# A state-space block and a mixture of experts on one core: the state's input product made in the router's pass and kept in DRAM

## The reference

```python
u = _rmsnorm(x, ssm_norm_w)
lam = jax.nn.sigmoid(log_lambda)
Bu = jnp.einsum('btd,nd->btn', u, B_w)
def step(h, bu_t):
    h = lam * h + bu_t
    return (h, h)
_, hs = jax.lax.scan(step, h0, jnp.swapaxes(Bu, 0, 1))
hs = jnp.swapaxes(hs, 0, 1)
y = jnp.einsum('btn,dn->btd', hs, C_w) + D_skip * u
x = x + y
z = _rmsnorm(x, ffn_norm_w)
gate = jax.nn.silu(jnp.einsum('btd,fd->btf', z, w1))
val = jnp.einsum('btd,fd->btf', z, w3)
```

## Time and profile before

| | us |
|---|---|
| median of 3 runs (1972.17 to 1979.03) | 1974.25 |
| the profiled execution | 1973.12 |
| its span, first to last instruction | 1971.2 |
| TensorE busy | 1804.0 |
| VectorE busy | 1038.4 |
| ScalarE busy | 652.8 |
| GpSimd busy | 1050.9 |

### The profile page before, as it was taken

One profiled execution on the slowest core, in us unless ns is written; L12 is line 12 of the kernel. 1 busy time (PEld: TensorE's weight loads), 2 busy tenths in 40 slices (PEclk: granted clock), 3 DMA queues, 4 the chain that ended last, 5 costly groups with the idle time before them and its releaser, 6 DMA issues.

```text
span 1971.2 us, 31040 instructions
## 1 busy us (share of the span) xinstructions
PE 1804.0 (92%) x9958; PEld 1346.9 (68%) x9960; DVE 1038.4 (53%) x2462; ACT 652.8 (33%) x1349; POOL 1050.9 (53%) x1057
## 2 busy tenths in 40 slices
PE   6798998999989999999999898888898869999995
PEld 3455555655568888889888787777787845555553
DVE  6587456333234555445455565566565635555554
ACT  5620222222224444444444343334343322222220
POOL 0003777777777777720004644445444157777666
PEclk9898999999989999999999999999999979999998
DMA  6804334563668889875557877777777653333333
GB/s 207 257 10 144 136 127 167 186 231 140 241 219 282 280 282 283 276 215 174 170 176 221 262 237 227 235 233 233 221 233 223 187 156 113 107 109 100 101 96 104
DMA packets 261671, 374.55 MB, mean 190 GB/s; under 512 B 30357, under 2 KB 227081, under 8 KB 260617
## 3 DMA queue, kind: packets, MB, share of 16 engines
q1 hardware_dynamic: 211448, 227.51, 37.5%
q0 software_dynamic: 49920, 145.03, 22.3%
q10 hardware_dynamic: 144, 0.03, 0.0%
HBM read 189.47 MB, written 182.98 MB: 189 GB/s over the span
## 4 chain that ended last, share of the span: by engine, by line
PE 66%; DMA 15%; DVE 12%; issue 3%; SPq 2%; ACT 1%; DVEq 1%; POOL 1%; POOLq 0%; ACTq 0%
PE ps L1155 21%; DMA arena<-sorted_rows 14%; PE ps L1239 14%; PE ps L1172 11%; PE ps L1253 9%; PE ps L1228 5%; DVE arena L1026 2%; DVE xe L940 2%; PE ps L1141 1%; PE ps L1112 1%; PE ps L1079 1%; PE ps L1128 1%; SPq L437 1%; DVE xe L941 1%; DMA big<-in_x 1%
## 5 line engine op out<-in xcount | busy, mean ns | idle before, releaser
L511 POOL DMA_INDIRECT xe<-results,slots x512 | 528.2, 1032 | 580.2 <-DMA results<-arena 252.1
L1239 PE MATMUL ps<-arena 128*128 128x128 f32 x4608 | 589.4, 281 | 41.9 <-DVE arena L1009 40.5
L1239 PEld LDWEIGHTS ps<-arena 128*128 128x128 f32 x4608 | 539.9, 193 | 111.1 <-ACT arena L634 60.6
L1155 PE MATMUL ps<-arena,w 128*128 128x512 f32 (+1 forms) x768 | 345.8, 593 | 0.0
L500 POOL DMA_INDIRECT sorted_rows<-big,slots x256 | 258.4, 1010 | 83.8 <-issue 77.7
L1253 PE MATMUL ps<-big,arena 128*128 x1152 | 297.7, 381 | 0.3 <-DVE arena L1017 0.3
L500 POOL DMA_INDIRECT sorted_rows<-xe,slots x256 | 252.9, 988 | 78.0 <-issue 78.0
L925 DVE TENSOR_TENSOR arena<-arena,ps 128x512 f32<-128x512 f32 (+1 forms) x128 | 87.8, 686 | 356.0 <-ACT arena L602 355.0
L602 ACT ACTIVATE arena<-ps 128x512 f32<-128x512 f32 (+1 forms) x128 | 76.3, 596 | 574.3 <-PE ps L1155 573.4
L1009 DVE COPY arena<-big 128x512 f32 x576 | 230.2, 441 | 64.4 <-issue 64.1
L639 ACT ACTIVATE arena<-ps 128x256 f32<-128x256 f32 x288 | 110.4, 383 | 423.2 <-PE ps L1239 423.2
(11 more groups left out here) (156 smaller groups left out, 1162.0 us busy)
## 6 DMA issues: line engine op xcount, KB each, us to landing
arena<-sorted_rows SPq DMA_DIRECT2D x288, 288.0 KB, 3.8
results<-arena SPq DMA_DIRECT2D x288, 256.0 KB, 2.6
big<-in_x SPq DMA_DIRECT2D x32, 512.0 KB, 4.3
sorted_rows<-big SPq DMA_DIRECT2D x2, 4608.0 KB, 23.9
xe<-results,slots POOLq DMA_INDIRECT x512, 3.2
out<-xe SPq DMA_DIRECT2D x64, 128.0 KB, 2.0
sorted_rows<-big SPq DMA_DIRECT2D x48, 144.0 KB, 1.8
big<-in_wexp SPq DMA_DIRECT2D x1, 5632.0 KB, 18.6
```

What stands on the lines that cost most here:

```text
L511: pool.indirect_dma_start(out=gathered_at[i % RING][:, k, :], out_offset=None, in_=results[half], in_offset=bass.IndirectOffsetOnAxis(ap=s ...
L1155: last = mm(ps[0:m, 2 + 2 * (s % 2) + u, :], w[:, u, c, lo:lo + m], src[:, c, :], start=c == 0, stop=c == DC - 1)
L1239: last = mm(ps[:, 2 + n % 2, (2 * s + u) * P:(2 * s + u + 1) * P], wgu[n % 2][:, s, at_w:at_w + INNER], rT[n % 2][:, (2 * s + c) * P:(2 * ...
```

## The change

The product with B is made in the router's pass, by the same matmuls that make the logits: the weights of both stand side by side in `first_w` (64 + 32 columns). ScalarE copies all 96 rows out, SyncE stores the 64 of the state to `bu_dram`, unscaled. 1/rms of each half of the tokens is made inside the pass (`rms_x`, `invert_rms_x`), turned by TensorE (`turn_rinv`), and stored to `rinv_dram`. For each group SyncE loads the product back (`bu`, 64 partitions of 512) and the factors, broadcast to 64 partitions, into the buffer `hs`; VectorE multiplies the two and scans from SBUF into `hs`. `bu_product`, `bu_scale` and `bu_transpose` go; the scan moves from s = 3 to s = 2 and the y product from s = 4 to s = 3. Two constants go to ScalarE's queue. The diff, cut:

```diff
-        bT = sb("bT", [P, DC, N_STATE])
+        first_w = sb("first_w", [P, DC, N_STATE + E])
-        gT = sb("gT", [P, DC, E])
...
+            def store_bu(g):
+                sp.wait_ge(a0_first_ready, g + 1)
+                sp.dma_start(bu_dram[g], a0_first[g % 2][0:N_STATE, :]).then_inc(bu_stored[g % 2], 16)
+
+            def load_bu(n):
+                sp.wait_ge(bu_stored[n % 2], 16 * (n // 2 + 1))
+                sp.wait_ge(rinv_stored, 16 * (n // 8 + 1))
+                if n:
+                    sp.wait_ge(y_ready, n)
+                sp.dma_start(bu, bu_dram[n]).then_inc(bu_loaded, 16)
+                sp.dma_start(hs, rinv_dram[n * GT:(n + 1) * GT, :].rearrange("t p -> (t p)").partition_broadcast(N_STATE)
+                             ).then_inc(bu_loaded, 16)
+
             for n in range(8):
                 load_x_a0(n)
+                if n >= 5:
+                    store_bu(n - 5)
...
             for n in range(8, GROUPS + 4):
                 load_x_a0(n)
+                if n < GROUPS + 3:
+                    store_bu(n - 5)
+                if n == 14:
+                    store_rinv(0)
+            load_bu(0)
+            for g in range(GROUPS - 2, GROUPS):
+                store_bu(g)
+            store_rinv(1)
...
+            load_bu(1)
             store_padding(0, range(E // 2))
             for g in range(FIRST - 1):
                 if g + 4 < FIRST:
                     sp.wait_ge(x_used, g + 1)
                     load_x(g + 4, g + 4)
                 store_part(g)
+                if g + 2 < FIRST:
+                    load_bu(g + 2)
...
+            sp.wait_ge(ey_act, ALL)
+            sp.wait_ge(ey_dve, ALL)
+            load_bu(FIRST)
             for g in LATE:
+                if g + 1 < GROUPS:
+                    load_bu(g + 1)
...
+                if g == 6:
+                    rms_x(0)
+                if g == 8:
+                    copy_rinv(0)
+                if g == GROUPS - 2:
+                    rms_x(1)
+            copy_rinv(1)
...
             def scan(n):
-                dve.wait_ge(buT_ready, n + 1)
-                nc.vector.tensor_tensor_scan(hs, lam_b[:, :], ps[0:N_STATE, 1, :], 0.0, ALU.mult, ALU.add
-                                             ).then_inc(hs_ready, 1)
+                dve.wait_ge(bu_loaded, 32 * (n + 1))
+                do(tt(bu, bu, hs, ALU.mult))
+                nc.vector.tensor_tensor_scan(hs, lam_b[:, :], bu, 0.0, ALU.mult, ALU.add).then_inc(hs_ready, 1)
...
                     if more and s == 2:
-                        bu_scale(g + 1)
-                    if more and s == 3:
                         scan(g + 1)
...
                 for c in range(DC):
-                    last = mm(ps[0:E, 4 + g % 2, :], gT[:, c, :], a0_xT[g % 2][:, c, :], start=c == 0, stop=c == DC - 1)
+                    last = mm(ps[0:N_STATE + E, 4 + g % 2, :], first_w[:, c, :], a0_xT[g % 2][:, c, :], start=c == 0, stop=c == DC - 1)
...
-                    if more and s == 2:
-                        bu_product(g + 1)
                     if more and s == 3:
-                        bu_transpose(g + 1)
-                    if more and s == 4:
+                        pe.wait_ge(xT_ready, g + 2)
                         y_product(g + 1)
```

More of the change, by code:

```diff
@@ L178, in build @@
         xT = take(DC * G).rearrange("p (c n) -> p c n", c=DC)
-        bu = take(GT * N_STATE).rearrange("p (t n) -> p t n", n=N_STATE)
+        bu = take(G)[0:N_STATE, :]
         hs = take(G)[0:N_STATE, :]
@@ L191, in build @@
         a0_xT = [take(DC * G).rearrange("p (c n) -> p c n", c=DC) for _ in range(2)]
-        a0_lT = [take(G)[0:E, :] for _ in range(2)]
+        a0_first = [take(G)[0:N_STATE + E, :] for _ in range(2)]
+        rinvT = take(P)[0:HT, :]
         at[0] = 0
@@ L282, in build @@
         block = ctx.enter_context(nc.Block())
-        CONSTS = 13
+        FIRSTS = 3
+        CONSTS = 11
         WEXP_LOADS = 1 + 1 + 4
@@ L620, in _ @@
             rms_z(0)
+            for par in range(2):
+                act.wait_ge(bu_stored[par], 16 * GROUPS // 2)
+            act.wait_ge(rinv_stored, 16 * HALVES)
             zT_copy(0)
@@ L711, in a0_normalise, with rms_x, invert_rms_x @@
                           ).then_inc(a0_xn_dve, 1)
+            def rms_x(half):
+                of = slice(half * HT, (half + 1) * HT)
+                do(tt(rinv[:, of], mv[:, of, 1], rstd[:, of], ALU.mult))
+                tt(rinv[:, of], rinv[:, of], rstd[:, of], ALU.mult).then_inc(ms_x_ready, 1)
+            def invert_rms_x(half):
+                of = slice(half * HT, (half + 1) * HT)
+                dve.wait_ge(rms_x_ready, half + 1)
+                nc.vector.reciprocal(rinv[:, of], rinv[:, of]).then_inc(rinv_ready, 1)
             for g in range(-4, GROUPS - 2):
@@ L717, in _ @@
                     a0_stats(g + 4)
+                if g == -3:
+                    dve.wait_ge(router_loaded, 16 * FIRSTS)
+                    for c in range(DC):
+                        last = tsc(first_w[:, c, 0:N_STATE], first_w[:, c, 0:N_STATE], ssmw_col[:, c:c + 1], None,
+                                   ALU.mult)
+                    last.then_inc(bT_folded, 1)
+                if g == 5:
+                    rms_x(0)
+                if g == 6:
+                    invert_rms_x(0)
+            rms_x(1)
+            invert_rms_x(1)
             def r_pairs(half):
@@ L969, in dve_group @@
                     route_late(g)
[L971 to L972 removed]
             dve.wait_ge(consts_loaded, 16 * CONSTS)
[L975 to L977 removed]
             do(nc.vector.memset(lam_b[:, :], 1.0))
             do(tt(skip_w[:, :], skip_w[:, :], ssmw_row, ALU.mult))
[L980 to L982 removed]
+            dve.wait_ge(rinv_ready, 2)
             dve.wait_ge(lam_ready, 1)
@@ L991, in _ @@
             make_z(0)
+            for par in range(2):
+                dve.wait_ge(bu_stored[par], 16 * GROUPS // 2)
+            dve.wait_ge(rinv_stored, 16 * HALVES)
             for g in range(FIRST):
@@ L1087, in a0_logits, with turn_rinv @@
                 for t in range(GT):
-                    last = tp(ps[:, 6 + g % 2, t * E:(t + 1) * E], a0_lT[g % 2][:, t * P:(t + 1) * P], ident[0:E, 0:E])
+                    last = tp(ps[:, 6 + g % 2, t * E:(t + 1) * E], a0_first[g % 2][N_STATE:, t * P:(t + 1) * P],
+                              ident[N_STATE:N_STATE + E, N_STATE:N_STATE + E])
                 last.then_inc(a0_logits_ready, 1)
             pe.wait_ge(consts_made, 1)
-            pe.wait_ge(router_loaded, 16)
+            def turn_rinv(half):
+                pe.wait_ge(rinv_ready, half + 1)
+                pe.wait_ge(logits_kept, 8 * half + 7)
+                tp(ps[0:HT, 6, 2 * P:3 * P], rinv[:, half * HT:(half + 1) * HT], ident[:, :]).then_inc(rinv_posed, 1)
+            pe.wait_ge(router_loaded, 16 * FIRSTS)
             a0_transpose(0)
+            pe.wait_ge(bT_folded, 1)
             for g in range(GROUPS):
@@ L1122, in transpose_z @@
                 transpose_group(z, zposed)
-            def bu_product(n):
-                pe.wait_ge(xT_ready, n + 1)
-                for t in range(GT):
-                    for c in range(DC):
-                        last = mm(ps[:, 0, t * N_STATE:(t + 1) * N_STATE], xT[:, c, t * P:(t + 1) * P],
-                                  bT[:, c, :], start=c == 0, stop=c == DC - 1)
-                last.then_inc(bu_ready, 1)
-            def bu_transpose(n):
-                pe.wait_ge(bu_scaled, n + 1)
-                for t in range(GT):
-                    last = tp(ps[0:N_STATE, 1, t * P:(t + 1) * P], bu[:, t, :], ident[:, :])
-                last.then_inc(buT_ready, 1)
             def y_product(n):
```

62 lines of the change are left out of this document (39 added, 23 removed).

## The result

The changed kernel takes **1982.52 us** (median of 20 runs, 1972.94 to 1991.48), the kernel before, run beside it, 1974.41: a ratio of **1.0036, 95% interval 1.0020 to 1.0051**. The forecast was 1977. The profiled execution took 1984.91, with a span of 1983.3 for 1971.2.

The account below looks back on a forecast made before the run. TensorE was taken to bound steady groups, busy 49.00 of 49 us, so 2.16 us a group counted in full. Terms summed to +3.0 on 1973.1, giving 1976.1, and with 1.1 about 1977 for the median; range 1965 to 1987.

Parts of the forecast that it names:

- the first rival: Clock falls in full: all four new TensorE waits cost 3.0 us, some 2 more in group 3; 1982 us, chance 0.17.
- the clock: TensorE at half rate behind new idle places: 2.5 us each in groups 0, 1, 3, 1.0 in group 4; +8.5.
- the start of group 0: Stretch to group 0: +6.4; within it, 0 for the serial product, scaling and turning that go, a gain up to 2.6.
- the term of group 1: Load for group 2 lands late in SyncE's queue, y waits 7.5 us: +8.9, from 6 to 10.
- Groups 0 and 3: TensorE's y product waits for VectorE's scan, about 4.4 and 4 us idle: +1.1 in each group.
- The load overtakes its queue: Rival: in group 1 the load lands at 183 instead of 186, 1974 us; chance 0.05.
- Stores in the queue of the router's pass: SyncE's stores delay constants and the ninth x load, +4.4; later x loads behind stores and an awaited square root, +2.0.
- the second rival: X loads pace the router's pass, taking 5.6 instead of 3.9 us, 5 us more: 1982 us, chance 0.12.
- Steady and late groups: No wait, 2.16 us saved a group: -8.6 over groups 2, 5, 6, 7 and -13.0 over six late groups.
- Wider product: Router product with 96 output columns for 32 costs nothing; 6 us if all 64 weight loads came into the open.
- Turn: Turn from experts to group 9: its load put at 1601, product and scan start to 1601.8; -1, from -2.5 to +1.
- Experts: Expert stretch: nothing changes but the date, they start later by about as much as the router's pass; 0 taken.

Follow-up runs that it names:

- e9: Changed kernel with early group 2 load, later y, stores on GpSimd, early group 9 load, plus unread products in waits starting groups 1 and 4: 1941.33 us.
- e1: Against the changed kernel, loads for group 2 go ahead of the padding, those of later early groups ahead of the part store: 1969.85 us, ratio 0.9981.
- e4: Against the changed kernel, the loads for group 9 are issued behind the first x load, ahead of three x and four part loads: 1974.95 us.
- e3: Against the changed kernel, the router pass's stores of the products and 1/rms leave from GpSimd's queue instead of SyncE's: 1976.37 us, ratio 1.0009.
- e2: Against the changed kernel, TensorE's y product stands one step later, as before the change: 1956.83 us, ratio 0.9917.
- e7: Changed kernel with 9, 23 and 8 unread products filling TensorE's waits in groups 0, 1 and 3, which was too many: 1983.14 us, ratio 1.0044.
- e8: Changed kernel with 5, 12 and 4 unread products filling TensorE's waits in groups 0, 1 and 3: 1975.34 us, ratio 0.9998.

## Why the prediction was right or wrong

The mechanism was right: what is saved in steady groups is given back in the router's pass, groups 0, 1 and 3. The time came out 5.5 us above the forecast, at the first rival's 1982. That it came so near is in part luck, for the terms missed to both sides: the clock was priced 4.8 us too low, the start of group 0 came 4.1 under its 6.4, and the term of group 1 holds 1.9 us twice.

- *The clock* is the term that was mis-sized. It was 2.5 us for each of groups 0, 1 and 3, 7.5 in all, from the place at the start of group 1; it measured 4.1 + 4.4 + 3.3 = 11.8. Group 4's 1.0 measured 1.5 (at 360.38 a down product of 3.44 us for 1.99, behind a wait of 3.44). Half of the time at half rate is lost. In the earlier trace rows the clock was 0.50 for 6.0 us behind the wait (153.80 to 159.82), and behind the y products for 8.5, 9.0 and 6.8; so the 3.0 from those rows was no bound. Why the clock came back later behind the y products isn't shown. Besides, e9 shows that the half rate at the start of group 1 costs nothing in the end, since VectorE is waited for next; behind a y product nothing gives it back. So the first rival, "the clock falls in full" beyond 3 us a place, describes what happened; its other 2 us, in group 3, didn't come (the +4.3 there is 1.1 and 3.3 of clock). The row that was held against it, a wait of 1.72 us with nothing lost behind it, has its opposite in the same trace: TensorE's timeline of group 1 before, then of the changed kernel, where a wait twice as long kept the full rate. The length of a wait alone doesn't tell whether the half rate follows.

```profile
173.81 3.50 PE L1172 MATMUL ps<-shd,arena 128*128 128x256 f32 x8 [1.70 <-DVE arena L925]
```

```profile
180.73 1.99 PE L1245 MATMUL ps<-shd,arena 128*128 128x256 f32 x8 [3.49 <-DVE arena L1008]
```

- *Groups 0 and 3*: y was to wait 4.4 and 4 us; it waited 4.40 and 3.94. Right.
- *Group 1*: y was to wait 7.5 us and waited 11.19. Counted from the start of the group (153.80 before, 161.95 now) the queue ran as the prediction put it: the part store moved by only 0.3 us, and the landing that it put at 186, which is 194.1 here, came at 195.2, 1.1 late. What failed is the step "TensorE came to that place at 180.58", 26.8 us into the group: it came after 24.2 (186.16), since the group's first products took 8.82 us for the 10.11 of the earlier trace rows and the down product of the rows above 1.99 for 3.50; the 1.73 of the product that went only lengthened the wait ahead of that down product, 3.49 us for 1.70. The 2.6 and the 1.1 make the 3.7 that were missing, and only the 1.1 costs time: what is gained ahead of a wait lengthens it. The +8.9 was also summed wrongly. At its 195.2 the y product is made, at the 186.27 of the earlier trace rows it is still to come, so y's 1.9 us stand in the difference; without them it is +7.0. Measured were 8.4 besides the clock. That the stretch cost 12.8 us for 11.4 is luck: the 1.9 too many stand against 1.1 of late landing and 1.9 of clock.
- *The load overtakes its queue*: not in group 1. The part store landed at 194.4 (188.28 + 6.1), the load at 194.9 (188.95 + 5.9). The Trainium skill's "DMA: Bandwidth & Descriptors" leaves such overtaking open ("Queues, rings and completion order"); these rows show none. At the end of the router's pass a load did land before an earlier one, but by 0.1 us (issued at 75.44 and 74.81, 4.3 and 5.0 us to landing). With nothing ahead of it in SyncE's queue the load is nearly as fast as this rival had it: in e1, issued at 128.38, it landed after 2.7 us. Behind others it took 4.5 us (e4) to 6.5 (the turn). The 2.3 us that the prediction gave as an estimate are worked out from "Anatomy of one DMA" on the same page of the Trainium skill, whose figures are for transfers that GpSimd issues; the 2.7 us come near it, the times behind others don't.
- *Stores in the queue of the router's pass*: the stall was to move by 4.4 and moved by 4.1. The +2.0 for x loads behind stores was wrong: VectorE's timeline of that pass shows two such waits after the ninth load, 0.31 and 0.19 us, and the turning of x for group 0 starts 3.2 later, not 6.4. So the second rival falls too.
- *Start of group 0*: 0 was taken; from the turning of x to y it is 6.47 us for 7.35, 0.9 gained, inside the bound of 2.6.
- *Steady and late groups*: 2.16 us each; 2.2 and 2.1 measured. Right.
- *Wider product*: nothing. Right, by e3, and by its own time: four of its records take 1.88 us at 61.28, for 1.90 at 61.82 before.
- *Turn*: -1 was taken, from -2.5 to +1. The profiled execution gave +2.0; e1, e2, e3, e7 and e8, which have the same turn, gave +0.1 to +0.5. The load came later than computed (1610.3 + 6.4 for its issue, then 9.4 to land), and what the serial product saved went there.
- *Experts*: 0 was taken, and the profiled execution gave +6.4, half of its whole loss. TensorE's waits for row loads in that stretch, before and after (us, times, longest):

```profile
PE ps L1228 <- DMA arena<-sorted_rows: 31.5, 54, 2.0
```

```profile
PE ps L1297 <- DMA arena<-sorted_rows: 40.3, 59, 2.4
```

No kernel edits the experts, and the eleven traces have them between 1018.9 and 1026.0. The profiled executions differ by 11.8 us and the medians by 8.1, so a part of it is that spread. Whether the change has a share in it stays open; it was not tried apart.

## What to carry to other kernels

Work that leaves the bound engine is worth its time only if every queue it moves to (SyncE's loads, the scan on VectorE) is ordered for it: here 2.16 us a group were real, and four orders hid them; mending these took 46 us off. That leaves 38 under the kernel before, more than the 30 of fourteen groups, since with the load in time the serial product is saved at the turn too (from the turning of x to y 3.21 us in e4, 9.77 before). Price a new wait of TensorE by what follows it: in full, with the half rate behind it, where TensorE then runs on, and without the half rate where it waits again. Take the half rate as the dear case: it didn't follow every wait.

## What the runs showed of the hardware

- Behind 3.94 to 11.19 us of idle TensorE, ahead of y, the next two products ran at half rate (1.2 GHz, a granted clock of 0.50 for 6.8 to 9.0 us), at a cost of 3.3 to 4.4 us; 11.19 us of waiting cost 0.3 more than 4.40. Ahead of the shared down product a wait of 1.70 us had the half rate behind it and one of 3.49 had not. Products that nobody reads, in the wait, kept the full rate (e7, e8).
- A load of 128 KB spread to 64 partitions landed in 2.7 us behind one other of 128 KB (e1, at 129.28), in 4.8 behind two and in 9.4 behind nine of 128 to 512 KB (e4 and the changed kernel): its place priced it, more than its shape.
- An f32 product of 512 columns is two records of 0.44 us in the trace; 9 products were 18 records (e7).
- GpSimd issued a plain store in 0.52 us, with no cost to the pass that it ran beside (e3).
